# Sum of squares in the two feed-forward blocks: two separate pair sums on POOL, added by PE in its accumulator

## What is computed

```
x = x + mamba(layernorm(x))         # selective scan, 256 channels, 16 states
x = x + ffn(layernorm(x))           # block "a"
x = x + min_gru(layernorm(x))       # 512 wide, gates z and h, a scan over the sequence
x = x + ffn(layernorm(x))           # block "d"
```

```
def _ternary_linear(x, w):
    ...
    rms = sqrt(sum(x * x, axis=-1)) / sqrt(d)
    x_norm = x / (rms + 1e-8)
    return einsum('bsd,fd->bsf', x_norm, w_q)
h = gelu(_ternary_linear(x, w_up))          # 512 wide
return _ternary_linear(h, w_down)
```

## Time and profile before

| | |
|---|---|
| runs | 866.34, 870.47, 874.72 us (median 870.47) |
| profiled execution | 870.38 us |
| its span | 868.6 us, 12461 instructions |
| mean granted clock of PE | 0.904 of full speed |

### The profile page before, as it was taken

The page is one execution under the profiler, slowest core; times in us unless marked ns, Lnnn a source line. Parts: engine busy times, 40 slices in busy tenths (PEclk is TensorE's granted clock), DMA queues, the critical chain, the costliest instruction groups (busy, mean ns, idle before and its releaser), DMA issues. The chain is left out here.

```text
span 868.6 us, 12461 instructions
## 1 busy us (share of the span) xinstructions
PE 706.7 (81%) x4060; PEld 594.6 (68%) x4060; DVE 677.0 (78%) x1059; ACT 641.6 (74%) x966; POOL 590.9 (68%) x375
## 2 busy tenths in 40 slices
PE   6446664789878997999788987999789977996975
PEld 5234553668767885778676876788667866785764
DVE  4379988869987998879977998799888997753231
ACT  4775669697789968996879778987898479616313
POOL 3178967776778877787868697888777576615312
PEclk9685776889989998999889998999899979999996
DMA  2541221112111211121111211121112111000000
GB/s 47 146 143 45 74 74 49 51 48 63 37 41 44 89 39 47 39 67 56 37 51 47 75 37 50 38 74 37 49 38 73 50 36 38 13 1 2 13 1 12
DMA packets 35185, 42.79 MB, mean 49 GB/s; under 512 B 7457, under 2 KB 17074, under 8 KB 35122
## 3 DMA queue, kind: packets, MB, share of 16 engines
q1 hardware_dynamic: 35122, 42.00, 15.9%
HBM read 39.63 MB, written 2.36 MB: 48 GB/s over the span
## 5 line engine op out<-in xcount | busy, mean ns | idle before, releaser
L441 POOL TENSOR_TENSOR inflow<-dtu,b_all 128x1024 f32<-128x1024 f32 x127 | 307.4, 2424 | 85.9 <-DVE state L1006 53.4
L1006 DVE TENSOR_TENSOR_SCAN state<-dA,inflow 128x512 f32<-128x512 f32 x256 | 298.4, 1207 | 31.2 <-ACT dA L771 27.8
L771 ACT ACTIVATE dA<-dt,decay_c 128x512 f32<-128x512 f32 x256 | 169.8, 685 | 56.6 <-DVE state L1006 55.7
L1023 DVE TENSOR_TENSOR state<-state,c_ps 128x1024 f32<-128x1024 f32 x128 | 155.5, 1215 | 22.4 <-PE c_ps L1305 18.8
L1314 PE MATMUL y_ps<-ident,state 128*128 128x128 f32 x1024 | 151.2, 297 | 0.0
L1314 PEld LDWEIGHTS y_ps<-ident,state 128*128 128x128 f32 x1024 | 135.7, 156 | 11.9 <-issue 3.8
L1201 PE MATMUL work<-in_hi,wzh_hi 128*128 128x512 f32 x256 | 103.6, 405 | 5.6 <-issue 4.3
L1305 PE MATMUL c_ps<-xd,pick 128*128 128x512 f32 x128 | 65.0, 508 | 46.0 <-DVE state L1023 45.7
L1203 PE MATMUL work<-in_lo,wzh_hi 128*128 128x512 f32 x256 | 101.0, 394 | 0.0
L1202 PE MATMUL work<-in_hi,wzh_lo 128*128 128x512 f32 x256 | 101.0, 394 | 0.0
L593 POOL TENSOR_TENSOR wide<-wide 128x512 f32<-128x512 f32 x48 | 61.1, 1273 | 27.5 <-ACT wide L818 25.0
(11 more groups left out here) (166 smaller groups left out, 1491.6 us busy)
## 6 DMA issues: line engine op xcount, KB each, us to landing
b_all<-b_scratch SPq DMA_DIRECT2D x128, 256.0 KB, 3.1
x_tok<-in_x SPq DMA_DIRECT2D x8, 256.0 KB, 3.8
out_x<-x_tok SPq DMA_DIRECT2D x8, 256.0 KB, 3.7
wide<-in_Wz SPq DMA_DIRECT2D x1, 1024.0 KB, 6.4
wide<-in_Wh SPq DMA_DIRECT2D x1, 1024.0 KB, 8.7
skip_f<-in_W SPq DMA_DIRECT2D x2, 256.0 KB, 5.7
dtu<-in_W_in SPq DMA_DIRECT2D x1, 256.0 KB
b_scratch<-gated SPq DMA_DIRECT2D x8, 32.0 KB, 1.6
```

The lines of the kernel that those rows point to most:

```text
L441: eng.tensor_tensor(inflow[:, n % 2, :, tok(b)], dtu[:, :, tok(b)], b_all[:, n % RING, tok(b)].unsqueeze(1).broadcast_to([P, HALVES, TO[b] ...
L771: act.activation(dA[:, h, tok(b)], dt[:, b % 2, h, tok(b)], ACT.Exp, scale=decay_c[:, h, n:n + 1]).then_inc(s_dA[h], 1)
L1006: dve.tensor_tensor_scan(state[:, g % 3, h, tok(b)], dA[:, h, tok(b)], inflow[:, n % 2, h, tok(b)], first, ALU.mult, ALU.add).then_inc(s_s ...
L1023: dve.tensor_tensor(state[:, g % 3, :, tok(b)], state[:, g % 3, :, tok(b)], c_ps[:, tok(b)].unsqueeze(1).broadcast_to([P, HALVES, TO[b] - ...
```

## The change

POOL adds block 1 to block 0 and block 3 to block 2, two adds that don't depend on each other, at the times of sum1 and sum3 in the table; sum2 is not used any more. PE waits for both, and for each tile of 128 tokens does two matmuls that accumulate in the same column of PSUM, one with the first sum as weights and one with the second. Nothing else is changed; lines below are shifted by two.

```diff
             def ffn_sum(t, c, k):
                 pool.wait_ge(s_sq[c], FB * t + k + 1)
-                if k > 1:
-                    pool.wait_ge(s_sqsum[c], 3 * t + k - 1)
-                pool.tensor_tensor(square[:, 0, tok(t)], square[:, 0, tok(t)], square[:, k, tok(t)], ALU.add
+                pool.tensor_tensor(square[:, k - 1, tok(t)], square[:, k - 1, tok(t)], square[:, k, tok(t)], ALU.add
                                    ).then_inc(s_sqsum[c], 1)
...
-                    for k in (1, 2, 3):
+                    for k in (1, 3):
                         for t in due(r, s, POOL_ON["%s.sum%d" % (c, k)]):
                             ffn_sum(t, c, k)
...
             def ffn_sumsq(t, c):
                 p = c + ".sumsq"
-                pe.wait_ge(s_sqsum[c], 3 * t + 3)
+                pe.wait_ge(s_sqsum[c], 2 * t + 2)
                 bank_free(t, p)
                 for j in tiles(t):
-                    last = pe.matmul(bank(p)[:, j:j + 1], square[:, 0, cols(j)], ones[:, 0:1], start=True, stop=True)
+                    for k in (0, 2):
+                        last = pe.matmul(bank(p)[:, j:j + 1], square[:, k, cols(j)], ones[:, 0:1], start=(k == 0),
+                                         stop=(k == 2))
                 last.then_inc(*made(p))
```

## The result

| | before | after |
|---|---|---|
| median of 6 runs | 870.41 us (866.34 to 875.53) | 899.04 us (893.44 to 901.73) |
| profiled execution | 870.38 us, span 868.6 | 893.44 us, span 891.6 |
| mean granted clock of PE | 0.904 | 0.887 |

The changed kernel takes 1.0313 times as long (95% interval 1.0265 to 1.036), some 27 us more. The forecast was 10.7 us more, 881.1 in all, with a range up to 886. The sign was right, the size was too small by 16.5 us.

The account below looks back on a forecast made before the run. It took PE's sum-of-squares group, not POOL's adds, to be on the path, no engine being the bound by itself. 6.2 + 0.65 + 2.6 + 0.4 + 0.9 = 10.7 us on 870.38 gave 881.1 us; range 873.5 to 886.

Parts of the forecast that it names:

- What bounds the kernel: At the changed places PE's sum-of-squares group is on the path and POOL's adds are not; removing 20.4 us of POOL costed at nothing.
- What is added: Sum-of-squares group on PE: eight more recorded matmuls, each with its own weight load at 0.112 us, 0.89 us per group.
- rival four: Added matmuls in the sum-of-squares groups take no time of their own, loads hidden under the 1.67 us wait: 871; chance 0.02.
- Sum by place: Delays added over eight "a" and eight "d" groups: 6.2 + 0.65 + 2.6 + 0.4 + 0.9 = 10.7 us.
- 7 x 0.89 = 6.2: "a" groups in rows 1 to 7 of x: the 0.89 us delay goes on in full at each, 6.2 us.
- 2.6 + 0.4 + 0.9 = 3.9: "d" groups: six places at 0.43 us, 2.6 in all; 0.4 at 803.48; 0.9 at the last, 861.47.
- 0.43 left after ACT's table load: Behind six "d" groups ACT's table load covers 0.46 of the 0.89 us; 0.43 goes on.
- Rival one: Delay partly absorbed in each row's stretch waiting for DVE: 5.0 to 8.1 us added, 875.4 to 878.5, named 876.5; chance 0.28.
- rival two: Lower PE clock catches four more sum-of-squares groups, each 0.65 us more, and some work beside them: 884 to 887; chance 0.08.
- rival three: Fewer POOL adds set DVE free, up to 20.4 us back against 10.7 lost: 860.7 us; chance 0.04.

Follow-up runs that it names:

- POOL's half alone: Against the kernel before, POOL does two adds in separate pairs, PE still four matmuls per group on the first sum only: 871.95 us, 0.9993.
- the wide kernels: 128 columns of ones as moving operand instead of one in all groups; against the kernel before, change in "a" alone 1.0019, in "d" alone 1.0004.
- the wide kernel before: The kernel before with 128 columns of ones as moving operand instead of one: 866.66 us, 0.9948; repeated 868.2 us, 0.9955.
- the wide pairs: The changed kernel with 128 columns of ones as moving operand instead of one: 876.86 us, 1.0041 of the kernel before; repeated 876.46 us, 1.007.

## Why the prediction was wrong in size

**What bounds the kernel: right.** PE's chain through the group, `c_ps` and the down-projection is on the path, and POOL's adds are not. POOL's half alone gives 0.9993.

**What is added, a group: right at the full clock.** 256 records, and 1.71 to 1.81 us from the start of the group to the next matmul at eleven of sixteen places (forecast 1.75 to 1.8). At 811.84 it is 1.84 without the wait behind it, at the last place 1.93, and the other three are the ones at the lower clock. The floor of 25 ns between matmuls, which the prediction has from the Trainium skill (TensorE: Matmul & The Clock Gate, "Back-to-back issue gap"), isn't the pace here, and rival four is out with it: 0.11 us for each record, with one column and with 128.

**Sum by place: right for own time, as far as the noise lets it be seen.** The sum said 10.7 us; without the clock's part 8 to 10 are measured. For "a" the forecast was 7 x 0.89 = 6.2; the wide kernels give 0.0019 + 0.0048 (from 0.9952 to 1.0019) = 0.0067, or 5.8 us. For "d" it was 2.6 + 0.4 + 0.9 = 3.9; they give 0.0004 + 0.0048 = 0.0052, or 4.5 us. The intervals leave each of the two open by 2 to 3 us, and the medians (875.93 and 873.24 against 866.66 us) give 9.3 and 6.6. The traces are sharper. Against the wide kernel before, the steps from "a" to "a" with the change in "a" alone grow by 0.93, 0.89 and 0.90 us where all groups have the full clock (0.89 forecast; by 1.43 in the fourth, which holds a slow group, and by 1.21 in the fifth), and with the change in "d" alone by 0.51, 0.51, 0.42 and 0.18 (0.43 forecast; the third step, 2.12, holds the slow group). And at the place shown above, from the "a" group at 630.64 to the "d" group at 647.05 it is 16.41 us in the wide pairs, and from 627.02 to 642.54 in the kernel before 15.52, so 0.89 more. Behind the "d" group, where I had 0.43 left after ACT's table load, DVE's wait for `c_ps` grows from 2.88 to 3.29 us, by 0.41. Rival one, a partial absorption, is not what these places show; by the total time alone its upper end (8.1 us) can't be told from the sum. One reading was loose: behind the "a" group of row 7 (792.29) there is no `c_ps`, and the step to PE's next product grows there from 1.82 to 2.19 us, by 0.37 and not 0.89.

**The step that failed: "One-column matmuls neither fill nor empty PE much, so I see no cause in the change", in rival two.** This put the chance of the lower clock at 0.08 and its price at "each costs 0.65 us more". Both were wrong, and so was the count of one caught group in sixteen: the one at 345.66 has the lower clock right behind it as well (granted 0.57 from 346.60 to 350.60). The change doubles just the kind of matmul behind which the clock falls, and the price is mostly not in the group but in the work behind it. At 638.73 the group costs nothing beyond its forecast; the down-projection costs 3.02 - 1.95 = 1.07 us and y_ps 1.66 - 1.04 = 0.62 us more. Between "a" and "d" the changed kernel takes 656.79 - 638.73 = 18.06 us, before 15.52: 2.54 more, of which 0.89 is own time. Behind "d" DVE's wait grows by 4.78 - 2.88 = 1.90 us and not by 0.41. From one column to 128 the changed kernel gains 21 to 24 us (1.0313 less 1.007 or 1.0041). The kernel before gains about 4 in the same way, so of the 27 us that the change costs, 8 to 10 are the matmuls' own time and 17 to 19 are the clock, for which my sum had 0.65. The rows to see it were at hand: at 438.67 I read the long group, charged it 0.65 us, and didn't read on to the 3.62 us of the down-projection at 440.77, which has the larger part of the loss at that place. (A smaller slip in the chances: by length seven tenths of the range from 877 to 884 lie above 879.1, and not five sixths.)

**Point by point, what I said would show it.** DVE's wait before ms_a grew from 12.6 to 17.8 us in all, 5.2 over eight places or 0.65 at each (forecast 0.9). POOL's before rms_a grew from 23.7 to 29.8 us, 0.8 at each where I said some 2: the freed time went to the waits before the adds, from 27.5 to 42.0 us in all, and not to the one before the root. 32 adds of 1274 ns and unchanged scans (1207 ns) put rival three out, and POOL's half alone, with nothing gained, shows it by itself. The distance from "a" to "a" grew by 2.72 us per row and not by 1.3: this is the reading that pointed to rival two.

**What stays open.** Why the clock falls behind one group and not behind the next of the same make. In the changed kernel it falls behind all six "a" groups of rows 1 to 6, but at the "d" groups of rows 0 to 5 only at 656.79 and 751.44; at 273.64, 368.60, 465.93 and 561.61 y_ps takes 1.07 us. I have no rule for it, and the profile's columns don't give one. The six timed executions of the changed kernel differ by 8 us with mean clocks from 0.879 to 0.887, the fastest with the highest; which groups are caught is known for the profiled one only. That a filled wait of 1.67 us before the "a" group would hold the clock was not tried, since the wait is for the only bank that the group may write.

## What to carry to other kernels

Before you add narrow matmuls to a busy PE, look at the granted clock and at the durations of the same-shaped matmuls right behind the ones that are there; price the change for that work too, and not for the added instructions alone. Where the weight load sets the pace, a wider moving operand costs next to no time (1.77 against 1.78 us for 16 records before `c_ps`, 1.86 against 1.78 at the "d" groups) and can hold the clock. And an addition taken from an engine that then waits for its input is worth nothing, however many microseconds of it there are.

## What was unexpected in the hardware

- 16 one-column records in an unbroken row (PE busy 1.77 of 1.80 us) are followed by a granted clock of 0.62, or 0.51 at the "d" group; 16 records of 128 columns in the same place as the first, at the same pace, by 1.00. Over all profiles, in the "a" groups of rows 1 to 6, the down-projection is slow behind 17 of 18 narrow groups of 16 records, behind 8 of 18 narrow groups of 8, and behind 1 of 42 wide ones.
- The fall comes behind the narrow group more than in it: 1.00 over the group at 638.70, 0.62 over the stretch from 640.80. In the changed kernel three of sixteen groups are slow themselves.
- The narrow column costs this kernel 21 to 24 of 899 us, although its mean granted clock is only 0.887 against 0.910 for the wide pairs (profiled executions).
- A float32 matmul with its own load of 128 x 128 weights takes 0.11 us per record whether 1 or 128 columns move, and the kernel before gets 0.5% faster by moving 128.
